# The token product of the next sequence in two halves, around the attention's first scores

## The reference

```python
# stage 1, on x: a linear map with modulated weights, heads attending to each other within a token
kx  = modulated_linear(x, s, k_aff_w, k_aff_b, k_w, k_b)        # the token product
kx  = kx.reshape(B, N, 16, 16)
A   = softmax(einsum('bnhd,bnjd->bnhj', kx, kx) / 4)
out = modulated_linear(einsum('bnhj,bnjd->bnhd', A, kx), s, o_aff_w, o_aff_b, o_w, o_b)
# stage 2: causal attention over the tokens with a bias, 16 heads of 16 features
logits = q @ k.T / 4 + incidence * decay ** distance * bias_scale
attn   = softmax(where(causal, logits, -inf))
out    = (attn @ v) @ w_out.T + b_out
# stage 3: layer norms with gathered gains, a gate, a router that sends each token to 2 of 8 experts
```

## Time and profile before

| | |
|---|---|
| median of 3 runs | 2396.26 us (2395.95 to 2396.81) |
| the profiled execution | 2401.86 us |
| its span | 2400.10 us |
| mean granted clock of TensorE | 0.909 of full |
| TensorE matmuls, weight loads | 2021.8 us, 1283.1 us |
| VectorE, ScalarE, POOL | 1325.6 us, 1003.4 us, 858.2 us |

### The profile page before, as it was taken

The page is one execution under the profiler, slowest core; times in us unless marked ns, Lnnn a source line. Parts: engine busy times, 40 slices in busy tenths (PEclk is TensorE's granted clock), DMA queues, the critical chain, the costliest instruction groups (busy, mean ns, idle before and its releaser), DMA issues. The chain is left out here.

```text
span 2400.1 us, 33909 instructions
## 1 busy us (share of the span) xinstructions
PE 2021.8 (84%) x11838; PEld 1283.1 (53%) x11838; DVE 1325.6 (55%) x3730; ACT 1003.4 (42%) x2505; POOL 858.2 (36%) x594
## 2 busy tenths in 40 slices
PE   5508889889889889899888898899999397979796
PEld 5305555555555465465555555557787154545454
DVE  2355757857867767678678545421111255555545
ACT  2105446646645655565466456231222041414141
POOL 0071725536447346356365320401000441515131
PEclk9658699998999989989999889899999698989998
DMA  7100021021030030030120220433354411102000
GB/s 266 47 0 21 1 61 40 1 91 27 1 107 12 12 97 10 19 100 1 58 60 1 81 71 1 138 104 136 132 187 145 143 36 41 49 28 61 19 13 19
DMA packets 67453, 146.09 MB, mean 61 GB/s; under 512 B 16356, under 2 KB 42074, under 8 KB 62946
## 3 DMA queue, kind: packets, MB, share of 16 engines
q1 hardware_dynamic: 51434, 93.79, 11.6%
q0 software_dynamic: 15872, 50.35, 7.5%
HBM read 114.64 MB, written 29.46 MB: 60 GB/s over the span
## 5 line engine op out<-in xcount | busy, mean ns | idle before, releaser
L1270 ACT ACTIVATE att_buf<-att_buf,nmin 128x384 f32<-128x384 f32 (+3 forms) x512 | 288.9, 564 | 379.3 <-DVE nmin L1642 379.1
L1043 PE MATMUL bank<-kk,qT 32*128 32x512 f32 (+2 forms) x1024 | 284.9, 599 | 37.3 <-DVE nmin L1642 36.8
L780 POOL TENSOR_TENSOR big<-ex_at,kx 128x2048 f32<-128x2048 f32 x64 | 236.7, 3730 | 133.5 <-DVE xt_na L1380 95.4
L1076 PE MATMUL bank<-ident,att_buf 128*128 128x128 f32 x1280 | 221.8, 300 | 50.3 <-ACT att_buf L1278 49.5
L727 POOL TENSOR_TENSOR big<-kx 128x1280 f32<-128x1280 f32 x64 | 162.5, 2574 | 160.7 <-ACT kx L1163 142.9
L1278 ACT COPY att_buf<-bank 128x384 f32<-128x384 f32 (+3 forms) x512 | 211.4, 413 | 17.3 <-PE bank L1090 15.7
L1631 DVE TENSOR_TENSOR att_buf<-bank,wdiag 128x128 f32<-128x128 f32 x384 | 93.0, 284 | 209.3 <-PE bank L1048 207.9
L1090 PE MATMUL bank<-att_buf,vp 128*32 128x128 f32 x2560 | 208.1, 297 | 0.0
L1076 PEld LDWEIGHTS bank<-ident,att_buf 128*128 128x128 f32 x1280 | 154.9, 154 | 70.2 <-ACT att_buf L1270 69.2
L792 POOL DMA_INDIRECT buf_d<-nB,sidx x64 | 62.6, 978 | 347.9 <-DVE sidx L1506 330.9
L1380 DVE TENSOR_REDUCE xt_na<-big 128x64 f32<-128x1024 f32 x128 | 152.2, 1213 | 13.4 <-POOL big L780 13.2
(11 more groups left out here) (356 smaller groups left out, 3983.2 us busy)
## 6 DMA issues: line engine op xcount, KB each, us to landing
big<-in_eW SPq DMA_DIRECT2D x16, 1024.0 KB, 7.7
kk<-in_eW SPq DMA_DIRECT2D x16, 1024.0 KB, 7.8
buf_d<-zero SPq DMA_DIRECT2D x8, 640.0 KB, 7.6
xt_na<-in_xT SPq DMA_DIRECT2D x8, 512.0 KB, 3.5
nA<-in_xN SPq DMA_DIRECT2D x8, 512.0 KB, 3.5
x_d<-x SPq DMA_DIRECT2D x8, 512.0 KB, 3.4
x<-x_d SPq DMA_DIRECT2D x8, 512.0 KB, 4.0
out<-qf SPq DMA_DIRECT2D x8, 512.0 KB, 2.9
```

The source lines that it names most:

```text
L780: pool.tensor_tensor(pv[:, c * P:(c + 1) * P, :].rearrange("p (h d) o -> p o h d", d=DH), spread(ex[:, t, :, 8 * c:8 * c + 8], 3, DH), spr ...
L1043: pe.matmul(bank[u % 2][:, 0:n], qT[r:r + 32, g, i * P:(i + 1) * P], kk[r:r + 32, g, T * i * P:T * i * P + n], start=True, stop=False)
L1076: mm = pe.transpose(bank[3 + u % 2][:, j * P:(j + 1) * P], pr[:, u % NPR, j * P:(j + 1) * P], ident[:])
L1270: act.activation(pr[:, u % NPR, 0:n], pr[:, u % NPR, 0:n], ACT.Exp, scale=-1.0, bias=nmin[:, u % 4:u % 4 + 1], accum_out=rsum[:, i, h:h + ...
```

## The change

The token product's stream on TensorE yields once more, between the blocks 1 and 2, with a place one higher than "kxmm" (-3), and TensorE's program runs what is due up to that place behind scores(0). So the first four matmuls stay where they were and the other four follow scores(0), ahead of the first unit. In a turn without stage 2 both halves run with nothing between them.

```diff
@@ token_stream of TensorE
                                     for t in range(T):
+                                        if t == T // 2:
+                                            yield AT["kxmm"] + 1
                                         for m in range(K2):
                                             mm = pe.matmul(bank[SIDE[t // 2]][:, (t % 2) * D:(t % 2 + 1) * D],
                                                            xT[:, m, t * P:(t + 1) * P], wk[:, m, :],
@@ the program of TensorE
                                 advance(side, AT["kxmm"])
                                 if b2 is not None:
                                     scores(0)
+                                    advance(side, AT["kxmm"] + 1)
                                 interleave(unit, side)
```

## The result

| | before | after |
|---|---|---|
| median | 2396.53 us (2395.95 to 2402.73, 4 runs) | 2376.44 us (2372.54 to 2382.28, 4 runs) |
| ratio | | 0.9912, 95% interval 0.9884 to 0.9941 |
| profiled execution, span | 2401.86 us, 2400.1 us | 2373.65 us, 2371.9 us |
| mean granted clock | 0.909 | 0.931 |

The change saves 20.1 us by these medians. A second measurement of the same kernel (e0_after, beside the 21 runs of before of the second batch) gave 2378.61 us against 2396.82, a ratio of 0.9939 (0.9920 to 0.9958), which is 18.2 us by the medians and 14.6 by the ratio. The forecast was 13.0 us. One execution of the later run e4 (2436.89 us) fell in a slower state and is left out of its figures.

What follows compares the result with a forecast made beforehand. The prediction saw three engines passing one baton in the attention's scores, with scores(0) held by the token product. Order 6.2 plus clock 6.8 gave 13.0 us, so 2396.26 - 13.0 = 2383.3 us, range 2375 to 2393.

Steps and rivals of the forecast that it cites:

- The order: Scores(0) follow half the product, held only by ScalarE's keys: 0.90 or 0.87 us earlier in seven sequences, 6.2 us.
- The second half under cover: The product's second half fits TensorE's idle 1.87 us ahead of scores(2): cost 0, with 0.05 us to spare.
- The clock: With that idle time filled, TensorE's half-clock stretches in the openings mostly go: 9.5 us counted, 6.8 taken.
- the discount: Two of seven sequences keep a half-clock stretch, as new idle time ahead of scores(0) can count: minus 2.7 us.
- The turn's end: The gain reaches the end, since POOL's last scatters start from sidx, which VectorE then makes earlier; no size of its own.
- Rival (a): Only the earlier scores(0) pays, the clock falls in all seven: 2390.1 us; 0.24, including part of the clock's gain.
- Rival (b): All half-clock stretches in the openings go, at the price of whole turns, 6.2 + 17 = 23 us: 2373; chance 0.06.
- Rival (c): The early gain is waited away at a gather or turn's end, or VectorE is not free: 2396.3 us; chance 0.11.
- Rival (d): New idle time ahead of scores(0) lowers the clock; 2 us lost per sequence, 14 in seven: 2410 us; chance 0.07.

Runs made afterwards that it cites:

- e0_after: The changed kernel unaltered, measured again as a base for its batch; 2378.61 us, ratio 0.9939 to before.
- e4: Changed kernel with the whole token product moved behind scores(0), none of it ahead; 2404.11 us, ratio 1.0031 to the kernel before.
- e7: Changed kernel with unit 0 in bank 2, so scores(0) waits only until VectorE has read that bank; 2376.95 us, ratio 0.9918 to before.
- e8: Changed kernel with two filler matmuls, read by nobody, behind TensorE's last work of each turn; 2381.76 us, ratio 0.9940 to before.
- e9: Changed kernel with two filler matmuls in mid-turn, between scores(38) and turn(36), where TensorE idles 1.40 us; 2370.83 us, ratio 0.9875 to before.
- e10: Changed kernel with two filler matmuls at the turn's end and two in mid-turn; 2366.37 us, ratio 0.9863 to before.
- e1: Changed kernel without the token product's second half in the seven turns that have an attention; 2403.57 us, ratio 1.0016 to before.
- e2: Whole token product ahead of scores(0) as in the kernel before, its second half computed once more behind them; 2379.13 us, ratio 0.9908 to before.
- e5: Changed kernel with five filler matmuls, read by nobody, behind TensorE's last work of each turn; 2391.49 us, ratio 0.9978 to before.
- e3: Changed kernel with three blocks of the token product ahead of scores(0) and one behind; 2374.38 us, ratio 0.9900 to before.
- e6: Kernel before, with five filler matmuls behind TensorE's last work of each turn; 2403.06 us, ratio 1.0034 to before.

## Why the prediction was right, and where by its steps it was not

The forecast of 2383.3 us, in a range of 2375 to 2393, met 2376.44: right in direction, mechanism and range, 7 us short of the gain.

1. **The order, 6.2 us forecast.** The step that failed is the release of scores(0). The prediction took ScalarE's keys as the only thing that holds them. Scores(0) wait as well (semaphore qk_ok, which the account of the kernel above leaves out) until VectorE's line 1598 is through with the queries and keys of the other groups, because unit 0's scores go to a bank that it reads. In before its row, which the prediction did not look at, ends at 360.47 + 2.20 = 362.67, 0.37 us behind the keys (362.30):

```profile
360.47 2.20 DVE L1598 TENSOR_TENSOR kk<-bank,rows 128x192 f32<-128x192 f32 x8
```

So scores(0) came 3.19 us behind the product's start (354.94 - 351.75) and not 2.75, and the gain was 3.65 - 3.19 = 0.46 us here. In the seven sequences it was 0.37 to 0.52, together 3.1 us in place of 6.2. e7 shows the missing part by taking this wait away. The rest of the step held: VectorE was free, and the gain passed to the minima (358.32 is 6.57 behind the start, 366.64 was 7.03).

2. **The second half under cover, 0 us, with 0.05 to spare.** Right, and as close as that: half done at 358.30, minimum at 358.32.

3. **The clock, 6.8 us of a counted 9.5.** The count was right; the discount, for two of seven sequences, was not paid in this profile. None of the seven sequences kept its stretch. (In the profiles of e8, e9 and e10 the same opening did have a fall behind the new idle time in 4 of 21 sequences, so the reason for the discount was sound.) The openings returned 13.3 us; less the order's 3.1, the clock gave 10.2 in them, against 3 x 1.26 + 7 x 0.81 = 9.5. ScalarE's wait of 0.81 us was indeed what gave way. In after the same copy has no wait ahead of it (first turn of the loop):

```profile
366.06 0.57 ACT L1281 COPY att_buf<-bank 128x512 f32<-128x512 f32 x1
```

366.06 - 351.75 = 14.31 us behind the product, against 547.02 - 531.34 = 15.68 before: 1.37 less, which is 0.46 of the order, 0.81 of the wait and 0.1 besides.

(The Trainium skill, "TensorE: Matmul & The Clock Gate", section "Why this matters for your kernels", warns only of idle gaps longer than 1.87 us, and by it the fill would return nothing. e1 and e2 decide against that reading for this kernel: with the gap open the clock fell within 10 us of the product's start in seven openings of seven, with the gap filled it held for these 10 us in seven of seven.)

4. **The turn's end.** Right: the wait for the last scatter is 5.33 us as before, and it starts earlier.

Rival (a), the order alone, is refuted: its order is worth 3.1 us at scores(0) and not 6.2, e1 has it with an open gap and gains nothing, and e2 has the gain in time without it. Rival (b) had the size, 17 us for the clock, but its reason was the price of the openings, and they gave 10.2. Rival (c) did not come. Rival (d) came in none of the seven sequences of after, at an idle time of 1.13 to 1.22 us where 0.9 was forecast. It is close, though: with 1.30 us in the same place it came in 4 of 10 openings (e5, e8, e9, e10).

**What stays open** is the part beyond the openings: 13.3 us are accounted for by rows, 18 to 20 were measured by the medians. In the profiled pair 15.2 us more were saved later in the seven turns and 8.7 lost at their heads, all in stretches at half clock that stand at other places than before. The same pattern of falls came in three profiled executions with a split product (after, e0, e3), seven turns of 1150.1 to 1150.2 us in each. Whether it follows from the change or is one of several patterns that the kernel can fall into was not told apart: the executions of after spread over 9.7 us and those of e0 over 13.7. The prediction had no term for it. Its 13.0 us stand against 13.3 in the openings, where two errors of about the same size, 3.1 us too much for the order and 3.4 too little for the clock, made up for each other: that the sum met the openings is luck. The 5 to 7 us beyond, by the medians, are this open part. By the ratio of the second measurement the whole gain is 14.6 us (10 to 19 by its interval), so the open part may also be as small as 1 us.

## What to carry to other kernels

Where TensorE's clock falls behind a short wait, look for independent matmuls to put into that wait, and count the gain by what waits for the slowed matmuls, not by TensorE's busy time: in the profiled pair TensorE was busy 40 us less and the span was 28 us shorter. When a piece of work is moved away from ahead of an instruction, list every semaphore that the instruction waits for and the end of each one's producer; the second latest takes over, here 0.4 us behind the first that was looked at. And keep a fill away from an engine's last work ahead of a barrier: five matmuls there cost 1.1 us a turn at the barrier, about what they had won at the turn's head.

## What the runs showed of the hardware that was not expected

- An idle time of 1.87 us (2.09 in the sequence ahead of the loop) on TensorE with the short scores around it had a fall of 6.8 to 13.7 us in it or within 2.1 us of its end in 19 of 21 openings (seven in before, seven in e1, five in e6). With 0.95 to 1.17 us ahead of scores(2) (e3), or 1.13 to 1.22 us ahead of scores(0) (after), no fall followed in seven of seven each; with 1.30 us ahead of scores(0) one did in 4 of 10 (e5, e8, e9, e10).
- Taking half of the product's matmuls away (e1) made the kernel no faster (1.0016) and its time at half clock longer, 239 us against 188. Adding a half (e2) left it at 0.9908.
- A fill of 1.1 us was enough (e3), and 4 more matmuls per turn in two other places brought a further 0.5 to 0.8% (e10, 0.9863 against 0.9912 in after and 0.9939 in e0), though each removed fall was in part given back by others.
- With the openings at full clock (after) five of the six turns of the loop became alike to 0.1 us, with the falls at the same places in each (440.5, 607.7, 775.0, 942.2 and 1109.5 us, each 167.25 us behind the last).
